# The low parts of the last table: five chunks one by one through PSUM, and a block that closes without GpSimd's drain

## The reference

```python
sp_emb = emb_tables[fidx, sp_input]            # 2048 x 26 x 32
lin_vals = lin_tables[fidx, sp_input, 0]
lin_output = ds_input @ lin_w.T + lin_b + jnp.sum(lin_vals, axis=1, keepdims=True)
s = jnp.sum(sp_emb, axis=1)
bi_pooled = 0.5 * (s * s - jnp.sum(sp_emb * sp_emb, axis=1))
x = jnp.concatenate([bi_pooled, ds_input], axis=1)      # 2048 x 45
h = jax.nn.relu(x @ w1.T + b1)                          # 256 wide
h = jax.nn.relu(h @ w2.T + b2)                          # 128 wide
out = jax.nn.sigmoid(h @ fw.T + fb + lin_output)
```

## Time and profile before

| | us |
|---|---|
| median of three runs | 391.92 |
| the profiled execution, its own time | 390.81 |
| its span, first to last instruction | 389.0 |
| PE busy | 383.0 (98%) |
| DVE busy | 334.3 (86%) |
| POOL busy | 285.3 (73%) |
| ACT busy | 251.0 (65%) |

### The profile page before, as it was taken

The page is one execution under the profiler, slowest core; times in us unless marked ns, Lnnn a source line. Parts: engine busy times, 40 slices in busy tenths (PEclk is TensorE's granted clock), DMA queues, the critical chain, the costliest instruction groups (busy, mean ns, idle before and its releaser), DMA issues.

```text
span 389.0 us, 5516 instructions
## 1 busy us (share of the span) xinstructions
PE 383.0 (98%) x1798; PEld 326.8 (84%) x1799; DVE 334.3 (86%) x349; ACT 251.0 (65%) x434; POOL 285.3 (73%) x308
## 2 busy tenths in 40 slices
PE   7999999999999999999999999999999999999996
PEld 3888888888888888888888888888888886668754
DVE  6699999989889796997969979698899899798843
ACT  5997767876466773865757656776567829552243
POOL 5777777777777777777777777777777777777770
PEclk9999999999999999999999999999999999999999
DMA  7833336332633327334263223622236222222220
GB/s 224 210 82 30 28 23 191 38 27 13 185 44 28 28 14 196 30 27 30 14 199 27 27 29 26 192 25 27 27 28 193 14 14 13 14 15 14 15 14 4
DMA packets 17125, 23.14 MB, mean 59 GB/s; under 512 B 6117, under 2 KB 16183, under 8 KB 16186
## 3 DMA queue, kind: packets, MB, share of 16 engines
q0 software_dynamic: 9536, 5.05, 22.7%
q1 hardware_dynamic: 7560, 17.73, 14.3%
HBM read 22.72 MB, written 0.04 MB: 59 GB/s over the span
## 4 chain that ended last, share of the span: by engine, by line
PE 94%; ACT 2%; DVE 2%; issue 1%; DMA 1%; DVEq 0%; ACTq 0%
PE cand L815 44%; PE cand L818 44%; PE bank_b L859 1%; PE cand L859 1%; DMA idx_raw<-sparse 1%; PE bank_b L869 1%; PE bank_b L875 1%; PE bank_b L837 1%; PE cand L869 1%; ACT gates L651 0%; ACT squares L676 0%; ACT h L703 0%; PE bank_a L837 0%; ACT high L618 0%; DVE x_and_y L493 0%
## 5 line engine op out<-in xcount | busy, mean ns | idle before, releaser
L343 POOL DMA_INDIRECT rows<-table,row_idx x293 | 279.6, 954 | 92.0 <-issue 69.5
L815 PE MATMUL cand<-high,gates 128*128 128x462 f32 x826 | 310.0, 375 | 0.3 <-DVE gates L394 0.3
L818 PE MATMUL cand<-low,gates 128*128 128x462 f32 x826 | 307.9, 373 | 0.0
L815 PEld LDWEIGHTS cand<-high,gates 128*128 128x128 f32 x826 | 155.8, 189 | 25.2 <-issue 6.9
L818 PEld LDWEIGHTS cand<-low,gates 128*128 128x128 f32 x826 | 155.4, 188 | 18.7 <-issue 0.7
L427 DVE TENSOR_REDUCE picks<-masked 128x66 f32<-128x924 f32 x56 | 107.6, 1921 | 1.9
L419 DVE TENSOR_TENSOR masked<-cand,mask 128x924 f32<-128x924 f32 x58 | 65.0, 1120 | 29.6 <-PE cand L818 29.2
L651 ACT ACTIVATE gates<-distance,one 128x512 fp32r<-128x512 bf16 (+1 forms) x124 | 80.9, 701 | 0.0
L643 ACT ACTIVATE distance<-codes,minus_key 128x512 bf16<-128x512 f16 (+1 forms) x120 | 78.4, 703 | 0.1
L394 DVE TENSOR_SCALAR gates<-bank_a,key_of 128x512 fp32r<-128x512 f32 (+1 forms) x86 | 58.8, 737 | 1.3 <-ACT bank_a L637 1.3
L631 ACT COPY bank_b<-high 128x462 f32<-128x462 f32 x42 | 23.1, 549 | 48.8 <-DVE low L406 48.0
(11 more groups left out here) (98 smaller groups left out, 109.7 us busy)
## 6 DMA issues: line engine op xcount, KB each, us to landing
stage<-tabs SPq DMA_DIRECT2D x7, 1617.0 KB
rows<-table,row_idx POOLq DMA_INDIRECT x293, 3.2
codes<-codes_dram SPq DMA_DIRECT2D x28, 128.0 KB
stage<-tabs SPq DMA_DIRECT2D x7, 231.0 KB, 4.2
idx_raw<-sparse SPq DMA_DIRECT2D x1, 208.0 KB, 2.6
w_sb<-w2t SPq DMA_DIRECT2D x1, 128.0 KB
dense_sb<-dense_cols SPq DMA_DIRECT2D x1, 120.0 KB
x_and_y<-dense_rows SPq DMA_DIRECT2D x1, 112.0 KB
```

Source lines behind the costliest of these rows:

```text
L343: pool.indirect_dma_start(out=to, out_offset=None, in_=table[:, :], in_offset=bass.IndirectOffsetOnAxis(ap=row_idx[:, at:at + 1], axis=0), ...
L815: first = nc.tensor.matmul(to, gate, high[f % 2][:, k, :], start=(k == 0), stop=False)
L818: last = nc.tensor.matmul(to, gate, low[f % 2][:, k, :], start=False, stop=(k == CHUNKS - 1))
```

## The change

Table 7 gets its chunks in another way. A new map, `LAST_AT`, gives chunks 0 to 3 to four places of job 24 and chunk 4 to the first place of job 25, one by one with `high_chunk` and `low_chunk`. Chunks 5 and 6 stay one piece, in job 26 as before.

```diff
--- before.py
+++ after.py
@@ -58,12 +58,11 @@
 
     FIRST_ACT = 2
 
-    PIECE = [0, 3, 5, CHUNKS]
-    PIECES = len(PIECE) - 1
+    SINGLE = 5
 
     def casts_until(f, k):
 
-        return CHUNKS * f + (k + 1 if f < MMF - 1 else sum(k >= c for c in PIECE))
+        return CHUNKS * f + (k + 1 if f < MMF - 1 else min(k, SINGLE) + 1)
 
 
     MUL, SHIFT = 293, 12
@@ -89,7 +88,10 @@
 
 
     CHUNK_AT = {(FIRST_OF[f - 1] + c // 2, c % 2): (f, c) for f in range(1, MMF - 1) for c in range(CHUNKS)}
-    CASTS = {FIRST_OF[MMF - 2] + g: (MMF - 1, g) for g in range(PIECES)}
+
+
+    LAST_AT = {(FIRST_OF[MMF - 2] + c // 4, c % 4): c for c in range(SINGLE)}
+    LAST_CAST = FIRST_OF[MMF - 2] + 2
 
     TILE_AT = {2 * t + 2: t for t in range(TILES - 5)}
     TILE_AT[NJ - 7] = TILES - 5
@@ -270,7 +272,7 @@
         y_made = sem("y_made")
         stored = [sem(f"stored{k}") for k in range(2)]
 
-        block = ctx.enter_context(nc.Block())
+        block = ctx.enter_context(nc.Block(no_gpsimd_drain=True))
 
         @block.sync
         def _(sp):
@@ -553,6 +555,8 @@
 
             for j in range(NJ - 2):
                 pick(j, 0)
+                if (j, 0) in LAST_AT:
+                    low_chunk(MMF - 1, LAST_AT[j, 0])
                 if j - 1 in SUMMED_OF:
                     b = SUMMED_OF.index(j - 1)
                     sum_pick_squares(b, 0, TB, MMF, b + 1)
@@ -564,6 +568,8 @@
                 make_gates(j + 2, 0, DVE_GATES[j + 2])
                 if (j, 0) in CHUNK_AT and CHUNK_AT[j, 0][1] < CHUNKS - 1:
                     low_chunk(*CHUNK_AT[j, 0])
+                if (j, 1) in LAST_AT:
+                    low_chunk(MMF - 1, LAST_AT[j, 1])
                 if j == NJ - 3:
                     sum_tile(TILE_IN[j])
                 if j in HIDDEN:
@@ -571,6 +577,8 @@
                 pick(j, 1)
                 if (j, 1) in CHUNK_AT:
                     low_chunk(*CHUNK_AT[j, 1])
+                if (j, 2) in LAST_AT:
+                    low_chunk(MMF - 1, LAST_AT[j, 2])
                 if j < BLOCKS - 1:
                     make_mask(j + 1)
                 if j + 1 in HIDDEN:
@@ -579,9 +587,10 @@
                     b = SUMMED_OF.index(j)
                     sum_picks(b, 0, TB, MMF)
                     add_dense(b, 2 * b + 1)
-                if j in CASTS:
-                    f, g = CASTS[j]
-                    low_piece(f, PIECE[g], PIECE[g + 1])
+                if (j, 3) in LAST_AT:
+                    low_chunk(MMF - 1, LAST_AT[j, 3])
+                if j == LAST_CAST:
+                    low_piece(MMF - 1, SINGLE, CHUNKS)
                 if j in TILE_AT:
                     sum_tile(TILE_AT[j])
                 if j == 5:
@@ -740,6 +749,8 @@
                 make_gates(j + 2, 0, FIRST_ACT)
                 if (j, 0) in CHUNK_AT:
                     high_chunk(*CHUNK_AT[j, 0])
+                if (j, 0) in LAST_AT:
+                    high_chunk(MMF - 1, LAST_AT[j, 0])
                 if j in HIDDEN:
                     relu1(HIDDEN[j], 0)
                 if j - 1 in SUMMED_OF:
@@ -748,14 +759,11 @@
                     relu1(HIDDEN[j], 1)
                 else:
                     make_gates(j + 2, FIRST_ACT, ACT_GATES[j + 2])
-                if j in CASTS:
-                    f, g = CASTS[j]
-                    if g == 0:
-
-                        act.wait_ge(stage_in, 16 * f)
-                        if f >= 2:
-                            act.wait_ge(gates_used, FIRST_OF[f - 1] * CHUNKS)
-                    high_piece(f, PIECE[g], PIECE[g + 1])
+                for at in range(1, 4):
+                    if (j, at) in LAST_AT:
+                        high_chunk(MMF - 1, LAST_AT[j, at])
+                if j == LAST_CAST:
+                    high_piece(MMF - 1, SINGLE, CHUNKS)
                 if (j, 1) in CHUNK_AT:
                     high_chunk(*CHUNK_AT[j, 1])
                 if j in TILE_AT:
@@ -808,7 +816,7 @@
                         pe.wait_ge(dve_gates, DVE_UNTIL[j] + k + 1)
                     else:
                         pe.wait_ge(act_gates, ACT_UNTIL[j] + (k - DVE_GATES[j]) + 1)
-                    if j == FIRST_OF[f] and (f < MMF - 1 or k in PIECE):
+                    if j == FIRST_OF[f] and (f < MMF - 1 or k <= SINGLE):
                         pe.wait_ge(low_made, casts_until(f, k))
                 to = cand[(PAIR[j] + i // 2) % CANDS][:, i % 2, 0:CS]
                 gate = gates[:, g % SLOTS, i * P:(i + 1) * P]
```

## The result

| us | before | changed |
|---|---|---|
| median of 20 runs each, on one chip | 391.38 | 390.03 |
| lowest to highest | 390.50 to 392.84 | 389.86 to 391.25 |
| the profiled execution, its own time | 390.81 | 390.37 |
| its span | 389.0 | 388.6 |

What follows compares the result with a forecast made beforehand. PE, busy 383.0 of 389.0 us, was taken as the bound. With a quick load, only the drain's 0.8 counted: span 389.0 to 388.2, median 391.92 to 391.1 us, 8-in-10 range 390.8 to 392.4.

Steps and rivals of the forecast that it cites:

- The drain: At the closing barrier: without GpSimd's drain SyncE arrives last and the span ends at 388.2, a gain of 0.8 us.
- The step that failed: GpSimd's gathers in jobs 24 to 26 end 1.34 us sooner, counted as worth nothing in the chain that ended last.
- The base: The profiled execution's 390.81 lay 1.1 under the median; the forecast took the median from 391.92 to 391.1 us.
- The rule on the shared interfaces: VectorE instructions with two SBUF inputs contend with GpSimd; by this alone earlier gathers would give the same 0.8 us.
- ScalarE and VectorE: Job 24: 6.0 us from load landing to chunk 1 shown, 0.55 more on VectorE; with a quick load PE does not wait.
- the signs: Job 24: a bracket of some 2 us ahead of ScalarE's chunk 0, under 0.6 us ahead of VectorE's chunk 1.
- Rival B: Last table's load takes 9.95 us, so PE stalls 1.05 us at job 26's layer 1: 392.2 us; chance 0.27.
- the point of 8.9: The load time in us from which PE was to wait at the first layer 1 product of job 26.
- Rival C: GpSimd's unfinished work is waited for behind the span anyway: 391.9 us, or 393.0 with a late load; chance 0.12.
- Rival D: VectorE's shorter queue behind `make_x` gives PE 0.3 us back: 390.8 us; chance 0.06 together with anything unseen.

Runs made afterwards that it cites:

- e2: The kernel before with only GpSimd's closing drain left out: median 390.86 us, ratio 0.9986; its profiled execution took 393.18 us.
- e1: The changed kernel with GpSimd's closing drain put back, so the chunks alone are changed: median 390.05 us, ratio 0.9973 to the kernel before.
- e6: The kernel before with one gather of tile 12 left out, drain kept: median 390.99 us, ratio 0.9970.
- e18: The changed kernel again, beside the kernel before on another chip: median 389.97 us, ratio 0.9980; its profiled execution took 390.84 us.
- e7: The changed kernel with four chunks one by one, chunk 1 behind job 24's second pick, three chunks left for job 26: median 390.37 us, ratio 0.9957.
- e3: The kernel before, unchanged, run again for a second profile: median 391.24 us, ratio 1.0008.
- e4: The changed kernel with the last table's load held back on SyncE until job 24: median 391.95 us, ratio 1.0033 to the kernel before.
- e8: e7 with the last table's load held back as in e4: median 390.64 us, ratio 0.9959 to the kernel before.
- e5: The changed kernel with GpSimd made later by three fills of an unused buffer ahead of tile 13: median 391.73 us, ratio 0.9990 to the kernel before.
- e17: The kernel before, old chunk order, with one gather of tile 12 left out and no closing drain: median 390.21 us, ratio 0.9984.

## Why the prediction was wrong

- **The drain: right in size.** With it left out, the span of the changed kernel is 388.2 without the start's 0.38, the lowest run of e2 is 0.70 under that of before, and where the kernel before has one group only the change is worth 0.82. But the changed kernel's last gather was issued at 377.95, so by the 10.0 us of e1 a drain would have ended at 387.95, ahead of SyncE's 388.3. In this execution the earlier gathers alone would have given nearly all of the 0.8; the two halves do not add.
- **The step that failed** is "That is worth nothing in the chain of the earlier trace rows, where no gather stands." The 1.34 us of the gathers was rightly counted for this execution and put at nothing. The last gather of the earlier trace rows, issued at 378.76, landed at 382.0, and ScalarE came for its rows at 382.15: a slack of 0.2 us. In e2, with the last gather 1.84 us later, PE waits, and the wait and the clock cost 2.4 us. The price of a gather that is a little later was never asked for. In its place the runs show a price near one to one: 1.13 us for one gather of 1.25 (e6), and no run of the chunks alone (e1) in the upper group, where the kernel before had 11 of 35.
- **The base.** "It lay 1.1 under the median, and the median goes from 391.92 to 391.1": the 1.1 was not an offset that stays. The three runs were all of the upper group, and that went away. Of the 1.09 us between 391.12 (391.92 less 0.8) and 390.03, 0.54 is that the kernel before itself has a median of 391.38 over 20 runs, and 0.55 that the change gained 1.35 and not 0.8. How much it gains depends on how many runs of the kernel before are long: 1.35 with 10 of 20, 0.82 with none.
- **The rule on the shared interfaces.** The long gathers under VectorE's subtractions with two SBUF inputs are gone with these, as the Trainium skill (GPSIMD Engine Reference, Specifications) has it. By that rule the drain could have stayed, and e1 bears it out with a ratio of 0.9973.
- **ScalarE and VectorE: right** in the sum from the landing, 6.5 us. `make_x` was 0.57 late; 0.45 was worked out for a load of 7.8 us, and this one took 8.02. Two of the signs did not come: the bracket ahead of chunk 0 was 2.90 and not some 2, and the one ahead of VectorE's chunk 1 was 0.90 and not under 0.6. PE did not wait all the same, as forecast.
- **Rival B, the late load: right in mechanism.** The stall was 0.79 in e18 at 9.87 us, where 1.05 was worked out for 9.95, and the point of 8.9 fits e1's 0.09 at 9.09. It was put at 0.27; 6 of 31 runs are long, one of them by a late load that is seen.
- **Rival C, GpSimd waited for anyway: wrong.** The time outside the span is 1.8 as before (390.37 less 388.6). The Trainium skill (Runtime: NRT & Kernel Launch, The ~15µs preamble/postamble breakdown) has a barrier of all engines behind each kernel. No row here shows it. If there is one, it added nothing to the 1.8 when GpSimd's drain was left out, and e2's lowest run, 0.70 under that of before, says the same.
- **Rival D** isn't seen: from the turn to layer 1 in job 26 are 3.92 us and 3.91 before, and from there to the chain at 375.51 are 53.92 and 53.93 before.

What stays open: why the kernel before has its upper group in nearly all, half, a third or none of its runs. The two pitches of the gathers, the start of GpSimd and the place of the gathers under the subtractions go the right way, but no upper run of the kernel before itself has a profile. By which way its gathers make them long, the landing and the clock or the drain's end, is therefore not shown. What makes the landing 3.2 us in some executions and 3.5 to 3.6 in others is not known either. Whether e7 beats the changed kernel isn't settled: they ran together only where PE paused. e7 is safer against a late load, but makes PE wait 0.39 us more with a quick one.

## What to carry to other kernels

A chain shows who arrived last, not who arrived second. Ask of each other engine's last transfer when it lands and when it is wanted, landing time included. Where that is under a few tenths of a microsecond, its engine is a second bound, and whatever lengthens or shortens its row has a price. When the runs before stand in two groups, find out in which of them the profile lies before forecasting from it, and what the other group waits for. And where an instruction waits for a load, put work that doesn't need the load ahead of it in the queue: chunk 1 one place later took the cost of a late load from 1.9 to 0.27 us. Look at what the new order makes wait, too: it cost 0.39 us at another place.

## What the runs showed of the hardware

- The last gather lands 3.2 us after its issue in the kernel before, e1, e3, e4, e7 and e8, and 3.5 to 3.6 after it in the changed kernel, e2, e5, e6, e17 and e18, though it brings 128 rows of 33 numbers only.
- A gather that begins under a VectorE subtraction with both inputs in SBUF takes longer by what is left of the subtraction, less 0.13 us (0.50 for 0.63 left, 1.36 for 1.49 left). One that begins ahead of it isn't lengthened.
- GpSimd's closing drain ended 9.9 to 10.0 us after the start of the last gather, in four profiles with it.
- The pitch of the gathers has two values, 1.249 and 1.251 us, each nearly constant in the middle of an execution. I don't know why.
- 1.36 us without work near the end of e2 were followed by a granted clock of 0.50 (1.2 GHz) until the end, which cost 1.25 us, more than the wait itself. After 0.61 and 0.54 us at the same place (e5, e6) the clock stayed at 1.00 until PE's work was done.
- The same load of a whole table took from 6.9 (e1's fifth) to 10.0 us from issue to use.
